# One decoder layer on one core: values of the cross part projected beside the first layer and kept in DRAM

## What is computed

```python
x = x + self_attention(layernorm(x))                  # 16 heads of 32, rotary, causal
x = x + cross_block(layernorm(x), ctx_2048)           # 16 heads of 128, 8 key groups
x = x + ternary_ffn(layernorm(x))                     # 2048 wide, weights quantized to -1, 0, 1 times a scale
# cross_block, of which the change touches the second line:
core = gqa(ln(fp8(h) @ wq), ln(fp8(h) @ wk), fp8(h) @ wv)
kx, vx = split(cond @ w_kv_x)                          # cond: 8 x 375 x 512, in f32
xout = gqa(ln(fp8(h) @ wqx), ln(kx), vx)
out  = fp8(concat(core, xout)) @ wproj
```

## Time and profile before

| | |
|---|---|
| median of 3 runs | 1212.75 us (1211.48 to 1212.91) |
| the profiled execution's own time | 1210.7 us |
| its span (first to last instruction) | 1208.9 us |
| instructions | 20265 |
| PE, DVE, ACT, POOL busy | 95%, 76%, 67%, 50% |
| HBM read, written | 62.78 MB, 8.39 MB |

### The profile page before, as it was taken

One profiled execution on the slowest core, in us unless ns is written; L12 is line 12 of the kernel. 1 busy time (PEld: TensorE's weight loads), 2 busy tenths in 40 slices (PEclk: granted clock), 3 DMA queues, 4 the chain that ended last, 5 costly groups with the idle time before them and its releaser, 6 DMA issues.

```text
span 1208.9 us, 20265 instructions
## 1 busy us (share of the span) xinstructions
PE 1145.5 (95%) x6270; PEld 764.5 (63%) x6330; DVE 919.6 (76%) x2801; ACT 810.7 (67%) x2316; POOL 607.7 (50%) x753
## 2 busy tenths in 40 slices
PE   4879989889999999999999999999999999999998
PEld 2557767556666665667666766667666666554564
DVE  4568978999878876898999999987787546586252
ACT  4667658777878876577667776678776678566140
POOL 1546985643544554464566655545543112257172
PEclk9989989899999999999999999999999999999999
DMA  8310110211211221213232232226111000000000
GB/s 274 89 60 24 27 34 17 87 54 55 69 36 36 62 83 48 93 37 102 92 113 84 73 93 74 79 74 204 61 44 52 1 1 1 2 1 1 35 1 27
DMA packets 30795, 72.48 MB, mean 60 GB/s; under 512 B 3184, under 2 KB 12528, under 8 KB 30688
## 3 DMA queue, kind: packets, MB, share of 16 engines
q1 hardware_dynamic: 30416, 70.82, 18.8%
q10 hardware_dynamic: 272, 0.36, 0.1%
HBM read 62.78 MB, written 8.39 MB: 59 GB/s over the span
## 4 chain that ended last, share of the span: by engine, by line
PE 61%; DVE 17%; ACT 10%; POOL 6%; issue 4%; DMA 1%; ACTq 0%; SPq 0%; POOLq 0%; DVEq 0%
PE ps L944 14%; PE ps L1041 8%; PE ps L1012 7%; PE ps L936 7%; PE ps L996 5%; PE ps L970 5%; PE ps L1053 4%; PE ps L979 3%; ACT big L1275 3%; PE ps L956 2%; DVE big L1414 2%; PE ps L863 2%; DVE big L1590 1%; ACT big L1334 1%; DVE big L1567 1%
## 5 line engine op out<-in xcount | busy, mean ns | idle before, releaser
L944 PE MATMUL ps<-big 128*125 128x512 bf16 x1152 | 264.7, 379 | 1.7 <-ACT big L1275 1.2
L1275 ACT ACTIVATE big<-ps,big 112x128 f32<-112x128 f32 (+1 forms) x512 | 192.8, 457 | 65.7 <-POOL big L1792 64.7
L944 PEld LDWEIGHTS ps<-big 128*125 128x125 bf16 x1152 | 155.1, 136 | 82.2 <-ACT big L1275 1.7
L1790 POOL TENSOR_TENSOR big<-big 112x4 f32<-112x4 f32 (+1 forms) x128 | 38.4, 300 | 321.6 <-ACT big L1107 321.5
L936 PE MATMUL ps<-big 128*112 128x512 bf16 x768 | 188.3, 389 | 1.8 <-ACT big L1309 0.8
L936 PEld LDWEIGHTS ps<-big 128*112 128x112 bf16 x768 | 100.4, 133 | 66.8 <-issue 7.6
L1334 ACT ACTIVATE big<-ps,big 112x375 f32<-112x375 f32 x128 | 74.6, 583 | 89.2 <-DVE big L1602 88.3
L1414 DVE BATCH_NORM_STATS2 big<-ps 112x6 f32<-112x128 f32 (+1 forms) x512 | 113.4, 285 | 20.9 <-PE ps L944 17.6
L996 PE MATMUL ps<-big 125*128 125x224 f32 (+1 forms) x512 | 121.3, 359 | 5.0 <-DVE big L1638 4.1
L1619 DVE TENSOR_SCALAR big<-big 112x112 f32<-112x112 f32 (+1 forms) x256 | 119.1, 486 | 6.8
L970 PE MATMUL ps<-big 128*112 128x375 f32 x256 | 102.1, 480 | 0.9 <-ACT big L1275 0.9
(11 more groups left out here) (124 smaller groups left out, 2312.4 us busy)
## 6 DMA issues: line engine op xcount, KB each, us to landing
big<-in_ctx_t SPq DMA_DIRECT2D x32, 375.0 KB, 3.4
big<-in_w_s SPq DMA_DIRECT2D x16, 512.0 KB, 3.8
big<-in_w_p SPq DMA_DIRECT2D x16, 512.0 KB, 4.1
big<-in_w_x SPq DMA_DIRECT2D x16, 512.0 KB, 3.8
big<-in_w_g SPq DMA_DIRECT2D x16, 512.0 KB, 4.2
scr<-big SPq DMA_DIRECT2D x36, 128.0 KB, 1.7
big<-scr SPq DMA_DIRECT2D x9, 512.0 KB, 8.2
big<-in_w_d SPq DMA_DIRECT2D x8, 512.0 KB, 4.2
```

Source lines behind the costliest of these rows:

```text
L944: t = e.matmul(bk[0:CK, :], ctxT[:, s, k, CK * c:CK * c + CK], wt[:, u, k, col:col + 512], start=k == s == u == 0, stop=k == 3 and s == 1)
L1275: t = e.activation(z[0:rows, 128 * j:128 * j + 128], ps(("p_mm", n))[0:rows, 128 * j:128 * j + 128], ACT.Identity, bias=v["q"][:, j:j + 1] ...
```

## The change

The cross part's values are no longer projected in the cross halves. In the cross halves `PROJ` has empty places (`None`) where three of the eight projections stood, and keeps eight ticks a batch. The 24 chunks of context (8 batches x 3) are loaded two at a time in the first layer's ticks and split once (`v_ld`, `v_in`). Both parts of a chunk are stored to DRAM (`v_cs`, tensor `cs`), and its values for both halves are projected (`v_mm`: 12 matmuls each, in three slots of four matmuls; a tick has four slots, ticks 8 to 15 five), copied out of PSUM by ACT (`v_ev`) and stored (`v_st`, tensor `vs`). Value weights get an input of their own, `w_v`, and are split in ticks 3 and 4 (`v_w`); they lie where S0's output projection goes, so S0's last eight units move from the first layer's ticks to a stream of their own at tick 42. In a cross batch SP loads the split context (`cs`, 768 KB into one buffer) at q0's tick and the values (`vs`, 768 KB) at k2's. X0's P^T copies go to ACT for every second head. Of the feed-forward's units 20 in place of 12 are made in X1, 28 in place of 36 are spilled, at six in place of eight per 16 ticks, and `b_back` moves from tick 146 to 160 of the loop. The S0 low parts that DVE made go to POOL. One empty place more stands before X0's attentions, and the last feed-forward steps go one tick later.

```diff
 A_PLAN = [
-    ("h", 2, "a_s2"), (8, "a_tq", 0), (9, "a_tq", 1), (6, "a_mm", 3), ("h", 2, "a_s2e"),
+    ("h", 2, "a_s2"), ("v", 0), (8, "a_tq", 0), (9, "a_tq", 1), (6, "a_mm", 3), ("h", 2, "a_s2e"),
     (5, "a_ev", 0), (6, "a_ev", 1), (7, "a_ev", 2), (5, "a_rot", 0), (7, "a_rot", 1),
-    (8, "a_te", 0), (9, "a_te", 1), (0, "a_ln", None), (0, "a_rstd", None),
-    ("h", 0, "a_qk"), ("h", 0, "a_s0"), (2, "a_tl", None), ("h", 4, "a_s4"),
+    ("v", 1), (8, "a_te", 0), (9, "a_te", 1), (0, "a_ln", None), (0, "a_rstd", None),
+    ("h", 0, "a_qk"), ("v", 2), ("h", 0, "a_s0"), (2, "a_tl", None), ("h", 4, "a_s4"),
     (A_LEAD + 7, "l_ln", None), (A_LEAD + 7, "l_rstd", None), (5, "a_mm", 2), (4, "a_mm", 1),
-    ("h", 3, "a_s3"), (A_LEAD + 9, "l_t", None),
+    ("v", 3), ("h", 3, "a_s3"), (A_LEAD + 9, "l_t", None),
     (A_LEAD + 10, "l_q", 0), (A_LEAD + 11, "l_q", 1), (A_LEAD + 12, "l_q", 2), (A_LEAD + 13, "l_q", 3),
-    (1, "a_tr", None), (3, "a_mm", 0), (0, "a_h", None), (A_LEAD + 7, "l_h", None),
+    (1, "a_tr", None), (3, "a_mm", 0), ("v", 4), (0, "a_h", None), (A_LEAD + 7, "l_h", None),
 ]
+N_CHUNK = 24
+V_FIRST, V_LAST, V_DENSE = 3, 43, range(8, 16)
+V_AT = {at: n for n, at in enumerate((tick, slot) for tick in range(V_FIRST, V_LAST) for slot in range(5)
+                                     if slot < 4 or tick in V_DENSE)}
+def early_values(at):
+    if at not in V_AT:
+        return
+    g = V_AT[at] - 4 * (6 - V_FIRST)
+    if g % 12 == 1 and (g + 11) // 12 < N_CHUNK // 2:
+        yield "v_ld", (g + 11) // 12
+    if g % 6 == 1 and 0 <= (g + 5) // 6 < N_CHUNK:
+        yield "v_in", (g + 5) // 6
+    if g % 6 == 0 and 0 <= g // 6 < N_CHUNK:
+        yield "v_cs", g // 6
+    for ahead, name in ((3, "v_ev"), (6, "v_st")):
+        n, part = divmod(g - ahead, 3)
+        if part == 0 and 0 <= n < 2 * N_CHUNK:
+            yield name, divmod(n, 2)
+    n, part = divmod(g, 3)
+    if 0 <= n < 2 * N_CHUNK:
+        yield "v_mm", (*divmod(n, 2), part)
 def first_layer(tick):
     for when, name, *more in A_PLAN:
+        if when == "v":
+            yield from early_values((tick, name))
+            continue
         if when == "h":
             name, lag = more[0], name
             g = tick - A_LEAD - lag
     out = []
     for h in HALVES:
-        seq = ["q0", "q1", "k0", "v0"] if h[0] == "S" else ["q0", "q1", "k0", "k1", "k2", "v0", "v1", "v2"]
-        out += [(h, b, s[0], int(s[1])) for b in range(NB) for s in seq]
+        seq = ["q0", "q1", "k0", "v0"] if h[0] == "S" else ["q0", None, "q1", "k0", None, "k1", "k2", None]
+        out += [s and (h, b, s[0], int(s[1])) for b in range(NB) for s in seq]
     return out
     out = []
     for h in HALVES:
         if h == "X0":
-            out.append(None)
+            out += [None, None]
         for b in range(NB):
             out += [(h, b, g, None) for g in range(4)] if h[0] == "S" else \
                 [(h, b, g, e) for g in range(4) for e in range(2)]
 PROJ, ATT = projections(), attentions()
 N_ITEMS = len(PROJ)
 ATT_N = [n for n, a in enumerate(ATT) if a is not None]
-FFN_DIRECT = 12
+FFN_DIRECT = 20
+N_BACK = (48 - FFN_DIRECT) // 4
+def half_units(h, *ranges):
+    return [None if h[0] == "X" and i < 16 and i % 4 == 3 else (h, i) for i in range(*ranges)]
 STREAMS = {
-    LEAD + 7: [("S1", i) for i in range(24)],
-    LEAD + 39: [("X0", i) for i in range(24)],
-    LEAD + 71: [("X1", i) for i in range(24)],
+    LEAD: half_units("S0", 16, 24),
+    LEAD + 7: half_units("S1", 24),
+    LEAD + 39: half_units("X0", 24),
+    LEAD + 71: half_units("X1", 24),
     64 + LEAD: [("F", i) for i in range(FFN_DIRECT, 48)],
-    LEAD + 135: [("F", i) for i in range(FFN_DIRECT)],
+    LEAD + 138: [("F", i) for i in range(FFN_DIRECT)],
 }
 def pace():
-    every = tuple(range(8))
-    beat = {LEAD + 7: every, LEAD + 39: every, LEAD + 71: (4, 5, 6, 7), 64 + LEAD: (0, 1, 2, 3),
-            LEAD + 135: (0, 1, 4, 5)}
+    every = tuple(range(16))
+    beat = {LEAD: every, LEAD + 7: every, LEAD + 39: every, LEAD + 71: (4, 5, 6, 7, 12, 13, 14, 15),
+            64 + LEAD: (0, 1, 2, 3, 8, 9), LEAD + 138: (0, 1, 2, 3, 8, 9, 10, 11)}
     when = {}
     for start, units in STREAMS.items():
         n, when[start] = 0, []
         while n < len(units):
             at = start + len(when[start])
-            pause = at < N_ITEMS - 16 and at % 8 not in beat[start]
+            pause = at < N_ITEMS - 16 and at % 16 not in beat[start]
             if pause or (n % 2 == 0 and at % 2):
                 when[start].append(None)
             else:
...
 def schedule():
-    s0 = [("S0", i) for i in range(24)]
+    s0 = half_units("S0", 16)
     def s0_ticks():
-        for t in range(25):
+        for t in range(17):
             if t >= 1:
-                yield [("b_1", s0[t - 1])] + ([("b_0", s0[t])] if t < 24 else [])
+                yield [("b_1", s0[t - 1])] + ([("b_0", s0[t])] if t < 16 else [])
             else:
                 yield [("b_0", s0[0])]
             yield "prep_a", 0
         if n == 3:
             yield "consts", 0
-        if n >= 6:
-            yield from next(prep, ())
-        if n >= 10:
+        if n in (3, 4):
+            for k in range(4 * (n - 3), 4 * (n - 3) + 4):
+                yield "v_w", k
+        if n >= 9:
             yield from next(prep, ())
     for rest in prep:
         yield from rest
     when = pace()
-    f_tick = [range(k, k + 5) for k in (-9, -8, -6, -5, 2, 9)] + [(16, 16, 17, 17, 18)]
-    for tick in range(N_ITEMS + 21):
+    f_tick = [range(k, k + 5) for k in (-9, -8, -6, -5, 3, 10)] + [(17, 17, 18, 18, 19)]
+    for tick in range(N_ITEMS + 22):
         yield from first_layer(T0 + tick)
...
     def is_tern(u):
         return u[0] == "F"
+    def ends_pair(u):
+        return u[1] % 2 == 1 or (u[0][0] == "X" and u[1] < 16 and u[1] % 4 == 2)
     def low_by_pool(u):
         name, i = u
-        return name != "F" and unit(u)[3] is None and not (name == "S0" and i >= 16)
+        return name != "F" and unit(u)[3] is None
...
+    def proj_before(h, b):
+        if b:
+            return proj_no(h, b - 1, "k", 2)
+        return proj_no("X0", NB - 1, "k", 2) if h == "X1" else proj_no("S1", NB - 1, "v", 0)
+    def x_free(h, b, last):
+        nb = NB * (h == "X1") + b
+        if nb == 0:
+            return [p_sum[proj_no("S1", NB - 1, "v", 0)]]
+        if nb == 1:
+            return [pv[att_no("S1", NB - 1)]]
+        hb = divmod(nb - 2, NB)
+        return [last[att_no(HALVES[2 + hb[0]], hb[1])]]
     def pT_by_act(n):
-        return ATT[n][0] == "X1"
+        return ATT[n][0] == "X1" or (ATT[n][0] == "X0" and ATT[n][3] == 1)
...
             if u[1] % 2 == 0:
-                stage_load(u, 1024, unit(u)[0])
+                stage_load(u, 512 if ends_pair(u) else 1024, unit(u)[0])
+        def v_w(i):
+            if i % 2 == 0:
+                stage_load(("v_w", i), 1024, w_v[i // 2])
+        def v_ld(m):
+            stage_load(("v_ld", m), 1000, ctx_t[m])
+        def v_cs(n):
+            w.wait_ge(*chunk_lo[n])
+            e.dma_start(cs[n // 3, :, n % 3, :], chunk_words[n % 3]).then_inc(
+                s_cs[n % 3].sem, 16)
+        def v_st(k):
+            n, h = k
+            w.wait_ge(*v_made[k])
+            e.dma_start(vs[h, n // 3, :, n % 3, :], v_out[h][0:CK, :]).then_inc(s_vs[h].sem, 16)
...
+            for j in range(N_BACK):
+                e.dma_start(f32(PW[1] + 256 * (FFN_DIRECT + 4 * j), 1024).rearrange("p (u w) -> p u w", u=4),
                             scr[4 * j:4 * j + 4].rearrange("u p w -> p u w")).then_inc(s_back.sem, 16)
         def p_mm(n):
             h, b, what, c = PROJ[n]
-            if h[0] == "X" and (what, c) == ("q", 0):
-                for i in range(2):
-                    stage_load(("p_mm", n, i), 750, ctx_t[b, :, 750 * i:750 * i + 750])
+            if h[0] == "S":
+                return
+            if (what, c) == ("q", 0):
+                for s in s_cs:
+                    w.wait_ge(*s[max(s.value)])
+                w.wait_ge(*p_sum[proj_before(h, b)])
+                e.dma_start(ctx_words, cs[b].rearrange("p c w -> p (c w)")).then_inc(s_ctx.sem, 16)
+            if (what, c) == ("k", 2):
+                for s in s_vs:
+                    w.wait_ge(*s[max(s.value)])
+                for free in x_free(h, b, pv):
+                    w.wait_ge(*free)
+                e.dma_start(vX[b % 2][0:CK], vs[int(h[1]), b]).then_inc(s_vx[b % 2].sem, 16)
         def d_1(b):
...
                 if n == 11:
                     t.then_inc(qkv_sum.sem, 1)
+        def v_mm(at):
+            n, h, part = at
+            bk = fresh(("v_mm", (n, h))) if part == 0 else ps(("v_mm", (n, h)))
+            w.wait_ge(*chunk_lo[n])
+            for m in range(4 * part, 4 * part + 4):
+                k, (s, u) = m // 3, ((0, 0), (0, 1), (1, 0))[m % 3]
+                w.wait_ge(*wv_lo[2 * k + h])
```

(32 more changed lines are left out.)

165 lines of the change are left out of this document (86 added, 79 removed).

## The result

The changed kernel takes **1290.36 us** (median of 4 runs, 1289.34 to 1292.26) against 1212.12 us of the kernel before on the same chip (4 runs, 1209.36 to 1212.91): a ratio of 1.066, 95% interval 1.0646 to 1.0673. It is 78 us slower; the forecast was 1207 us. The profiled execution is the slowest of the four (1292.26), so that its stages add up to 81.5 us.

A forecast was written before the change was run, and what follows sets the result against it. PE was taken to bound the cross halves, busy 591.0 of 600.5 us. Early side +101.6, cross part -108.4 and an extra tick +1 gave -5.8 on the profiled execution, so 1207 us, range 1183 to 1230.

The forecast's parts named there:

- The removal: Cross halves: 576 value matmuls at 0.216 us leave, and PE gives back their whole time, -124.2 us.
- DVE's balance: X0: DVE's 29.5 us a batch about equal PE's, so 1.6 us a batch added, by S0's six per cent; X1 nothing.
- The loads: Cross halves: context, value and weight loads on SP may reach ACT late; +3 us, bounds 0 and 32.
- the mark of 15 us: Cross halves: ACT waiting over 15 us for context, value or weight loads would show rival (b).
- (b): Cross halves: loads stall ACT, 2 us at each of 16 batches, giving 1236 us; chance 0.15.
- The early side: First layer with the moved products: tick 42 moves from 201.2 to 302.8, +101.6 us, bounds +86 and +112.
- The start: Before tick 7: value-weight loads and splits move it from 29.3 to about 36.8 us, bounds 31 and 40.
- The rest: One extra tick where S1 gives way to X0 and at the end: +1 us, between 0 and 4.
- (a): Both sides pack fully: early ticks run at 256 us and DVE keeps up in X0; 1184 us, chance 0.22.
- (d): The two sides cancel, the first layer being as full as the cross halves: 1212 us, chance 0.08.
- (c): X0: DVE and POOL block each other, +15 us on the forecast, 1222 us; chance 0.10.
- the cross halves give less than 90: Sign that the forecast is wrong: the cross halves give back under 90 us, where -108.4 was forecast.

The follow-up runs named there:

- Experiment 1: The kernel before with the cross values' 576 matmuls and their copies left out and nothing put early: 1182.60 us against 1209.93.
- experiment 5: The changed kernel without the feed-forward's ternary units, constants standing in for those weights: 1218.81 us.
- experiments 13: The changed kernel without ternary units, but with DVE's five instructions of each unit at their old ticks, on their own data, waiting for nobody: 1253.76 us.
- experiment 14: The changed kernel without ternary units, but with DVE's five and POOL's two instructions of each unit, on their own data: 1284.84 us.
- experiment 8: The changed kernel with the same ternary units spread evenly over the ticks, each a tick or more apart: 1262.79 us.
- experiment 3: The changed kernel with split context loaded for the first cross batch alone and values for the first two: 1283.09 us.
- experiment 15: The kernel before with its context split once beside the first layer, stored and reloaded; values still projected in the cross halves: 1235.44 us, ratio 1.0212.
- experiment 9: The changed kernel with ternary units spread evenly, and the value weights split one tick later (ticks 4 and 5): 1258.20 us.
- experiment 12: The kernel before with its ternary units at every second tick and recalled four ticks later: 1227.42 us, ratio 1.0133.

## Why the prediction was wrong

**The step that failed** stands in its first part: "So moved PE work gives its whole time back in the cross halves". It was drawn from a busy share of 98% and from waits of 3.2 us. Both are true of a stretch in which PE and DVE are full in turn; neither tells what happens when PE's part of it shrinks. Experiment 1 takes the very work out and gets 27.3 us of 124, and from the batches without a ternary unit 5.6 to 7.2 of 7.8 each.

**The removal, -124.2.** The size of the work was right: experiment 5 gives 125.6 us back, after its one load wait is taken off, and no more than 11 of these can be the units' own. What was missing in the sum is what stood beside it.

**DVE's balance, +1.6 us a batch of X0, none in X1.** This is the term that was mis-sized: with 124.2 out and 7 to 14 for the loads, the measured 36.8 leave 73 to 80 us for it, where the sum had 13. Neither its place nor its form held. It was put into X0 alone, but X0 missed by 13 us and X1 by 58. And the sum compared DVE and PE over a batch, 29.5 against 30.2 us, and took S0's six per cent for the loss. But PE and DVE do not even out over a batch here. The list puts an attention's steps a fixed number of ticks apart, and to a large part each tick costs its longer side (225 of 236 us and 269 of 284 when cut so, experiment 1; that the buffers are what forbids more was not tried). The changed kernel's DVE is busy only 212.4 of 272.2 us in X0, and PE waits for it all the same. The sum had no term for the clock either: up to 24 us of the 87 that were kept back. Nearest to a decomposition of the 71.5 us (84 without the filling's wait) that the ternary units cost are experiments 13 and 14: DVE's own instructions 35, POOL's 31 to 36, and the rest (their chain through ACT, their loads and stores) 6 to 13, not told apart further. Cut the other way, their placing is worth 28 (experiment 8). X1 missed by most, -2.4 for -60.6: at 26.2 of 29.8 us DVE was taken to cost nothing, but X1 took over eight units from X0 (28 mask steps start in it in place of 20, and 20 in X0 in place of 28). The sum took one unit a batch off X0 and put none into X1. X1's batches with four or five units took 32.9 to 43.9 us, the one with two 30.0.

**The loads, +3 (bounds 0 and 32).** Measured 7, in the cross halves alone 14 (experiment 3). ACT's waits passed the mark of 15 us set for rival (b), its rows in the cross halves being

```profile
ACT big L1464 <- DVE big L1736: 102.7, 52, 4.6
...
ACT big L1378 <- DMA big<-in_w_g: 8.1, 2, 6.5
ACT big L1378 <- DMA big<-in_w_p: 7.0, 2, 3.6
ACT big L1378 <- DMA big<-in_w_x: 3.6, 2, 1.8
```

18.7 us for weight loads, yet the run says 7 to 14: the first row, ACT's exp waiting for DVE's maximum, is the wait that matters.

**The early side, +101.6 (bounds 86 and 112).** Measured +112.1. The packing of ticks 7 to 41 was right: 268.0 us for 266, with PE busy 262.8 and the clock at 0.98, and with it the reading that a period of 17.4 us held 16.4 of work. That the splits and stores cost nothing on top was not a matter of course: without the products beside them they cost 30 us (experiment 15). The start was off: tick 7 at 45.3 for 36.8 (bound 40). The sum had the eight pieces of splits one behind the other, but PE also waited 10.1 us behind them for the second batch; a tick's delay of the splits gives 4.6 back (experiment 9).

**The rest, +1 (bounds 0 and 4).** +5.3. The last projection of X1 ends one place earlier than before, since the last place is empty, so part of it may be only the border that moved; the rest was not looked into.

**The rivals.** (a) fell, and (d) too: the sides cancel only in a kernel without ternary units (experiment 5 less its own wait, 1206 us). (b) is real at 7 to 14 us. (c) is real in mechanism, at 31 to 36 us in experiments 13 and 14, but not as what the forecast lacked: it stood for more blocking than in the kernel before, and the division took 665 ns in the changed kernel against 657, the mask step 712 against 792. Its mark (the mask step over 950 ns) shows in experiment 14 alone; the division (534 to 665 ns) would have been the better one, being the step that PE waits for. The Trainium skill (SBUF — State Buffer, "SBUF: two separate sides") lets GpSimd's instructions and those of VectorE with two SBUF inputs or in a two-port mode exclude each other, and no others; the runs agree in that the maximum and the copy, which read PSUM, are untouched, and show for the division and the mask step a mean lengthening of 25 and 41%. None of the rivals was at 1290 us, since all of them, too, added whole-batch sums. The mark "the cross halves give less than 90" was the one that caught it; the other, over 112 us more in the early stage, was just reached (112.1).

What stays open: what the lower clock would give back by itself (directly at most 25 us), the last 6 to 13 us between experiment 14 and the changed kernel, why the same spreading costs the kernel before 17 us (experiment 12), and which step makes the holes in the first layer of experiment 15.

## What to carry to other kernels

An engine at 98% without waits can still be one of two that are full in turn: before counting on the time of work to be taken away, cut the windows as finely as the order of the work is tied (here the tick, not the batch or the stage), and add up for each the longer side of what is left. Then take the work out by itself in one run and move it only if that run gives the time; here one kernel would have shown 27 us to be had for 102 to be paid by the forecast's own count. And when work leaves a tick, look at what was scheduled beside it because it was there: the heavy steps of the second engine have to be placed anew, and the placing measured: spreading them gave 28 us in the changed kernel and cost 17 in the kernel before.

## What the runs showed of the hardware that was not expected

With POOL given more to do on SBUF (118 to 207 us busy of 430), two kinds of DVE instruction that stay in SBUF took 25 and 41% longer (534 to 665, 692 to 979 ns), and those that read PSUM did not change (530 to 529, 480 to 479 ns). Both are means over two sorts: with no POOL instruction beside it a division took 415 or 416 ns in four kernels and a mask step 692 or 693, with one 603 to 763 and, where POOL was given more, 1193. The quantization's steps remained at 278 ns, most of them with POOL idle; but 12 of one of them (L1814 in experiment 14) had POOL at work beside them and took 278 as well.

A hole of 5.1 us in PE's work (634.1 to 639.3) was followed by a granted clock of 0.63 over the next 4 us, although DVE, ACT and POOL were at work all the time. The cross halves of the changed kernel have ten stretches at 1.2 GHz, 51 us in all; each began in a hole of PE or less than 1 us behind one. As an estimate, half of such time is what it costs: that is 20 of the 31 us of experiment 14 and 19 of the 30 of experiment 15.

Twelve issues on SP, one behind the other, that repeat a small constant block over the weights held its queue for 27.3 us, 2.3 us each (experiment 5), and the changed kernel's seven recalls from DRAM 14.2 us, 2.0 each, where a single issue in the same timelines takes about 0.3. So it is not the repeating that makes them long; what does was not tried.
